# Expert feed-forward stages: the tile code rolled into hardware loops, rows staged by ScalarE, landings counted by SyncE, and the last stage's additions issued at other steps

## The chip, the cores and the metric

The kernel runs on one core of one Trainium2 chip. Its engines are TensorE (PE; PEld is its weight load), VectorE (DVE), ScalarE (ACT), GpSimd (POOL) and SyncE (SP), each with an instruction stream of its own; they meet through semaphores. The metric is device time in microseconds, lower is better; the median of three runs is what counts.

## The reference

A two-layer decoder on x of 64 x 64 tokens of 128 values (4096 tokens, so 32 token tiles of 128). Each layer is a sequence mixer, a cross attention and a mixture-of-experts feed-forward stage. Only the two feed-forward stages are touched:

```python
# layer 0: gate by sigmoid, two of eight experts, plus two shared experts
top_w = softmax(gathered);  h_r = gelu(x @ Wfc_r[e].T);  expert_out = h_r @ Wproj_r[e].T
return x + shared_out + routed_out
# layer 1, the last stage: gate by softmax, two of eight experts, with biases
for e in range(8):
    h = gelu(x @ W1[e] + b1[e]);  y = h @ W2[e] + b2[e]
    output = output + y * combine_w[..., e:e + 1]
```

## The kernel before

`ffn_phase` is built twice, as f0 (layer 0) and f1 (layer 1, the last stage). It sends every token row to its two experts by sorting:

- **Routing.** DVE works out for each token and choice the slot of its row. Slots are grouped in tiles of 128 rows, each tile owned by one expert (`owner[0, tile]`). Tokens are cut in two parts of 20 and 12 token tiles, which need 47 and 31 slot tiles: M = 78. `hot(q)` writes, for a group q of four token tiles, two one-hot arrays (`hot_tile`, times the token's number, and `hot_row`), and PE multiplies them (`collect(q)`) into the table `source` of rows by slot. Groups 0 to 4 belong to part 0. Groups 5 to 7 (part 1) are made at steps `HOT_LATER` of the tile loop.
- **Rows in.** POOL fetches 128 rows for each slot tile with an indirect DMA (`f_xn<-f_xn_rows,f_source`, L1616) into a ring of 32 tiles, in lots of 1, 1, 2 and then 4. A lot may start when the tile 32 places back has been read. Below, a *burst* is a run of such DMAs issued one behind the other.
- **Tile steps.** A Python loop over s = 0..79 writes out every step. PE transposes tile s (L1956), multiplies tile s-1 by the up weights (four matmuls, L1963) and tile s-2 by the down weights (four, L1975). DVE copies the transposed rows from PSUM (`xT`, L1797), adds the up bias in f1 (L1802), and writes y of tile s-2 (L1817; with its bias L1815 in f1). ACT does gelu (L1880) and copies the owner's up weights into a ring of three (`w_tile`, L1868). Each engine reads the tile's owner into a register with a TENSOR_LOAD (L1542) and addresses weights or biases by it.
- **Rows out.** SP stores y two tiles at a time. When part 0 is stored, POOL gathers the results back to token order, eight indirect DMAs for each group m (L1627, `f_hot_row<-f_slots_y,f_slots`), and DVE adds them with their weights (`add_rows`, L1560), in four quarters. Two buffers hold groups m and m+1, so the gather of group m+2 waits until group m is added. Groups 0 to 2 are added at steps `ADDED_AT` and the three after each, the others behind the loop. Group 5 is the first that needs part 1.

```python
        for s in range(M + 2):
            if s in lot_of: pe.wait_ge(landed[n], ...)   # PE itself waits for the lot's landing
            pe.transpose(bank_x[s % 2][:, 0:P], x_in[:, s % RING, :], g.ident[:])
HOT_LATER = (4, 10, 16)
ADDED_AT = (63, 69, 75)
```

Of the kernel before, what the change touches and what calls it, by code (L numbers as in the profile page):

```python
# [23 lines left out]
ALU = mybir.AluOpType  # L24
AXIS = mybir.AxisListType

P = 128
# [1305 lines left out]
W_RING = 3  # L1333
# [94 lines left out]
def ffn_phase(g, name, spec):  # L1428
# [14 lines left out]
    RING = TILES  # L1443
    lots = [(start[part] + begin, size) for part in range(parts)
            for begin, size in in_lots(counts[part], (1, 1, 2, 4) if part == 0 else (4,))]
    lot_of = {begin: n for n, (begin, _) in enumerate(lots)}
    stores = [(part, begin, size) for part in range(parts) for begin, size in in_lots(counts[part], (STORED,))]
    store_of = {start[part] + begin + t: n for n, (part, begin, size) in enumerate(stores) for t in range(size)}
    stores_of = [sum(1 for part, _, _ in stores if part < upto) for upto in range(parts + 1)]
    with ExitStack() as ctx:  # L1450
# [22 lines left out]
        def lent(n, shape, dt=F32):  # L1473

            if not following:
# [22 lines left out]
        xT = [sb(f"xT{k}", [D, P]) for k in range(2)]  # L1498
        w_tile = [sb(f"w_tile{k}", [D, FFN]) for k in range(W_RING)]
        hidden = [sb(f"hidden{k}", [P, FT, P]) for k in range(2)]  # L1500
        y_out = [sb(f"y_out{k}", [P, STORED, D]) for k in range(Y_RING)]
# [12 lines left out]
                 "owner_ready", "hot_ready", "hot_used", "source_ready", "xT_in_psum", "xT_ready",  # L1514
                 "w_ready", "up_done", "biased", "hidden_ready", "y_in_psum", "y_ready")
        S = {k: g.sem(f"{name}_{k}") for k in names}
        stored = [g.sem(f"{name}_y_stored{k}") for k in range(Y_RING)]
# [22 lines left out]
        def owner_of(kind, tile):  # L1540

            _, (value,) = nc.values_load_multi_w_load_instructions(  # L1542
                owner[0:1, tile:tile + 1], engines=(kind,), min_val=0, max_val=EXPERTS - 1,
                skip_runtime_bounds_check_because="a minimum with EXPERTS - 1 bounds them")
            return value
# [17 lines left out]
        def stores_done(eng, upto):  # L1563

            for k in range(Y_RING):
                need(eng, stored[k], 16 * len(range(k, upto, Y_RING)))

        statistics = RowStatistics(g, name, ctx)
        with nc.Block() as block:  # L1569

            @block.sync
            def _(sp):
# [6 lines left out]
                for n, (part, begin, size) in enumerate(stores):  # L1579
                    sp.wait_ge(S["y_ready"], start[part] + begin + size)  # L1580
                    sp.dma_start(slots_y[part].rearrange("(j p) d -> p j d", p=P)[:, begin:begin + size, :],
                                 y_out[n % Y_RING][:, 0:size, :]).then_inc(stored[n % Y_RING], 16)
# [10 lines left out]
                stores_done(sp, len(stores))  # L1593

            @block.gpsimd
            def _(pool):
# [5 lines left out]
                if spec["plus_xn"]:  # L1602
                    for q in range(GROUPS):
# [15 lines left out]
                for m in range(GROUPS):  # L1619
                    part = max(p for p in range(parts) if first_group[p] <= m)  # L1620
                    if m in first_group:
                        stores_done(pool, stores_of[part + 1])
# [10 lines left out]
            def _(dve):  # L1633
# [95 lines left out]
                def hot(q):  # L1729
# [7 lines left out]
                    seq(dve.tensor_tensor(out, tile_numbers[:, 0:N].unsqueeze(1).unsqueeze(1).to_broadcast(shape),  # L1737
                                          tile_of[:, :, at].unsqueeze(3).to_broadcast(shape), ALU.is_equal))
                    dve.tensor_tensor(out, out, token_rows[:, at].unsqueeze(1).unsqueeze(3).to_broadcast(shape),
                                      ALU.mult)  # L1740
# [51 lines left out]
                for s in range(M + 2):  # L1792
                    if biased and s < M:
                        held[s] = owner_of(mybir.EngineType.DVE, s)
                    if s < M:
                        dve.wait_ge(S["xT_in_psum"], s + 1)
                        dve.tensor_copy(xT[s % 2][:], bank_x[s % 2][:, 0:P]).then_inc(S["xT_ready"], 1)  # L1797
                    m = s - 1
                    if biased and 0 <= m < M:
                        dve.wait_ge(S["up_done"], m + 1)  # L1800
                        shape = [P, 1, FT, P]
                        dve.tensor_tensor(before_gelu[m % 2][:].unsqueeze(1),  # L1802
                                          bank_h[m % 2][:].rearrange("p (o j t) -> p o j t", o=1, t=P),
                                          b_up[:, bass.ds(held[m], 1), :].unsqueeze(3).to_broadcast(shape), ALU.add)\
                            .then_inc(S["biased"], 1)
                    m = s - 2
                    if 0 <= m < M:
                        dve.wait_ge(S["y_in_psum"], m + 1)
                        n = store_of[m]
                        at = m - start[stores[n][0]] - stores[n][1]  # L1810
                        if at == 0:
                            need(dve, stored[n % Y_RING], 16 * (n // Y_RING))
                        y, out = bank_y[m % 2][:, 0:D].unsqueeze(1), y_out[n % Y_RING][:, at:at + 1, :]
                        if biased:
                            ins = dve.tensor_tensor(out, y, b_down[:, bass.ds(held.pop(m), 1), :], ALU.add)  # L1815
# [3 lines left out]
                    if parts > 1 and s in HOT_LATER:  # L1819
                        hot(first_group[1] + HOT_LATER.index(s))  # L1820
                        if s == HOT_LATER[-1]:
                            sources(1)
                    if parts > 1:
                        for m, begin in enumerate(ADDED_AT):
# [258 lines left out]
```

## Time and profile before

| | us |
|---|---|
| median of 3 runs (1453.18 to 1457.63) | 1457.05 |
| the profiled execution, its own time | 1444.6 |
| its span, first instruction to last | 1442.8 |
| PE busy in it | 1175.6 (81%) |
| DVE busy | 829.6 (57%) |
| ACT busy | 649.3 (45%) |
| POOL busy | 600.1 (42%) |

The profiled execution is one run with the trace on; it lies 12.4 us under the median of the timed runs. Its span is what the rows below add up in. In these rows names are given without buffer numbers and without the digit of f0 and f1: f0's tile steps lie between 288 and about 515 us, f1's between 1139 and 1393 us.

### The profile page before, as it was taken

What the parts mean: (1) busy time and instruction counts of PE and PEld (TensorE: products, weight loads), DVE (VectorE), ACT (ScalarE), POOL (GpSimd) and SP (SyncE); (2) the same over time, 40 slices, a digit from 0 to 9 for tenths busy, and PEclk for the clock granted to TensorE, in tenths of its full rate; (3) what the DMA queues carried; (4) which work ended last, traced back from release to release, by engine and by line L of the source; (5) the groups of instructions that cost most, each with busy time, mean ns of one, the idle gap of its engine ahead of it and who ended that gap; (6) DMA issues with size and microseconds to landing.
All of it is one profiled execution on the core that took longest, in us unless ns stands there. A gap on an engine that the chain in (4) does not pass through costs nothing. (4 is left out here: it accounts for less than half of the span.)

```text
span 1442.8 us, 31655 instructions
## 1 busy us (share of the span) xinstructions
PE 1175.6 (81%) x11702; PEld 988.7 (69%) x11702; DVE 829.6 (57%) x1805; ACT 649.3 (45%) x1171; POOL 600.1 (42%) x622
## 2 busy tenths in 40 slices
PE   6979989919996889689999999968997718886840
PEld 4766666819996867468888888856767718885840
DVE  6859978403221324358888888847986615553541
ACT  5327754304453424155666656536772103452410
POOL 4742323264444235544343433333342463444255
PEclk9999998959997999899999999999997959997975
DMA  6002215012221121100000000001105011221122
GB/s 171 9 2 66 51 24 202 14 46 49 57 65 47 46 85 32 44 6 1 0 0 0 0 0 0 1 6 19 21 9 196 25 45 43 60 58 46 42 79 69
DMA packets 61906, 62.62 MB, mean 43 GB/s; under 512 B 12592, under 2 KB 50864, under 8 KB 61296
## 3 DMA queue, kind: packets, MB, share of 16 engines
q1 hardware_dynamic: 51824, 42.52, 9.9%
q0 software_dynamic: 9088, 18.63, 5.2%
q8 instruction: 61, 1.00, 0.3%
q14 instruction: 37, 0.30, 0.1%
q10 hardware_dynamic: 896, 0.17, 0.1%
HBM read 42.67 MB, written 16.52 MB: 41 GB/s over the span
## 5 line engine op out<-in xcount | busy, mean ns | idle before, releaser
L1963 PE MATMUL f_bank<-f_xT,f_w_tile 128*128 128x128 f32 x1248 | 184.5, 295 | 82.7 <-issue 48.1
L1963 PEld LDWEIGHTS f_bank<-f_xT,f_w_tile 128*128 128x128 f32 x1248 | 167.7, 208 | 88.9 <-issue 50.8
L1975 PE MATMUL f_bank<-f_w_down,f_hidden 128*128 x1248 | 179.2, 290 | 50.8 <-ACT f_hidden L1880 30.0
L1975 PEld LDWEIGHTS f_bank<-f_w_down,f_hidden 128*128 128x128 f32 x1248 | 162.6, 203 | 56.4 <-issue 56.2
L1616 POOL DMA_INDIRECT f_xn<-f_xn_rows,f_source x156 | 148.6, 952 | 47.4 <-issue 47.4
L1424 POOL TENSOR_TENSOR f_turn_cell<-ident 128x1 f32<-128x1 f32 x60 | 12.8, 213 | 319.5 <-issue 107.1
L1627 POOL DMA_INDIRECT f_hot_row<-f_slots_y,f_slots x128 | 122.6, 958 | 39.9 <-issue 39.9
L1050 POOL TENSOR_TENSOR ret_rstd<-ret_var,ret_minus_half 128x8 f32<-128x8 f32 x32 | 52.7, 1647 | 173.5 <-DVE ret_var L1089 173.5
L1880 ACT ACTIVATE f_hidden<-f_before_gelu 128x512 f32<-128x512 f32 x78 | 49.0, 629 | 162.0 <-DVE f_before_gelu L1802 146.4
L1880 ACT ACTIVATE f_hidden<-f_bank 128x512 f32<-128x512 f32 x78 | 46.5, 596 | 149.5 <-remote 83.9
L1868 ACT ACTIVATE f_w_tile<-f_w_up 128x512 f32 x156 | 96.2, 619 | 29.0 <-DVE f_owner L1768 28.2
L885 PEld LDWEIGHTS a_mixed_psum<-a_v_diag,a_probT 128*64 128x64 f32 x2048 | 65.8, 138 | 59.4 <-ACT a_probT L837 43.7
L1817 DVE COPY f_y_out<-f_bank 128x128 f32<-128x128 f32 x78 | 22.7, 291 | 138.9 <-PE f_bank L1975 100.0
L788 DVE TENSOR_REDUCE a_top<-a_scores 128x16 f32<-128x1024 f32 x64 | 78.4, 1224 | 37.5 <-PE a_scores L870 36.5
L747 POOL TENSOR_TENSOR X<-X,a_mixed 128x128 f32<-128x128 f32 x64 | 29.2, 456 | 160.6 <-DVE a_mixed L780 160.1
L837 ACT ACTIVATE a_probT<-a_probT_psum 128x1024 f32<-128x1024 f32 x64 | 65.5, 1024 | 57.6 <-PE a_probT_psum L896 57.6
L1053 POOL TENSOR_TENSOR ret_qk<-ret_qk,ret_turned 128x1024 f32<-128x1024 f32 x32 | 76.3, 2386 | 25.2 <-DVE ret_turned L1109 25.1
L1802 DVE TENSOR_TENSOR f_before_gelu<-f_bank,f_b_up 128x512 f32<-128x512 f32 x78 | 53.8, 689 | 52.0 <-PE f_bank L1963 28.9
L791 DVE TENSOR_TENSOR a_prob<-a_scores,a_top 128x1024 f32<-128x1024 f32 x64 | 78.4, 1224 | 2.2
L885 PE MATMUL a_mixed_psum<-a_v_diag,a_probT 128*64 128x18 f32 x2048 | 71.3, 212 | 7.9 <-ACT a_probT L837 5.9
L896 PE MATMUL a_probT_psum<-ident,a_prob 128*128 128x128 f32 x512 | 70.8, 282 | 5.9 <-ACT a_prob L811 5.9
L1258 PE MATMUL ret_ps<-ret_wo,ret_gated 128*128 128x128 f32 x512 | 67.1, 285 | 4.9 <-DVE ret_gated L1081 4.8
(283 smaller groups left out, 2827.8 us busy)
## 6 DMA issues: line engine op xcount, KB each, us to landing
f_slots_y<-f_y_out SPq DMA_DIRECT2D x76, 128.0 KB
a_v_rows<-in_ctx SPq DMA_DIRECT2D x16, 256.0 KB, 4.0
f_xn_rows<-f_xn SPq DMA_DIRECT2D x16, 256.0 KB
f_w_up<-in_f_up SPq DMA_DIRECT2D x1, 2560.0 KB, 10.1
f_w_down<-in_f_down SPq DMA_DIRECT2D x1, 2560.0 KB, 17.1
f_xn<-f_xn_rows,f_source POOLq DMA_INDIRECT x156
X<-in_x SPq DMA_DIRECT2D x4, 512.0 KB, 5.3
kv_ctxT<-in_ctxT SPq DMA_DIRECT2D x8, 256.0 KB, 5.7
```

The costliest lines, as they stand in the source:

```text
L788: dve.tensor_reduce(top[b][:], bank_s[b][:], AXIS.X, ALU.max).then_inc(S["top_ready"], 1)
L791: dve.tensor_tensor(prob[b][:], bank_s[b][:], top[b][:].unsqueeze(2).to_broadcast([P, HEADS, SEQ]), ALU.subtract)\
L885: last = pe.matmul(bank_o[64 * row:64 * row + 64, 18 * hp:18 * hp + 18], probT[b][:, hp, 64 * row:64 * row + 64], v_diag[octet][:, 2 * (tu ...
L896: last = pe.transpose(bank_t[:, hp, :], prob[b][:, 2 * hp:2 * hp + 2, :].rearrange("p h t -> p (h t)"), g.ident[:])
L1053: pool.tensor_tensor(qk[k % 2][:], qk[k % 2][:], turned[k % 2][:], ALU.add)\
L1258: last = pe.matmul(ps_vg[:, 0:D], gated[b][:, h, :], wo[:, h, :], start=(h == 0), stop=(h == H - 1))
L1616: pool.indirect_dma_start(out=x_in[:, s % RING, :], out_offset=None, in_=xn_rows[:, :], in_offset=bass.IndirectOffsetOnAxis(ap=source[:, s ...
L1627: pool.indirect_dma_start(out=rows[m % 2][:, t, n, :], out_offset=None, in_=slots_y[part][:, :], in_offset=bass.IndirectOffsetOnAxis(ap=sl ...
L1868: nc.scalar.activation(w_tile[s % W_RING][:].unsqueeze(1), w_up[:, bass.ds(expert + E0, 1), :], ACT.Copy)\
L1880: nc.scalar.activation(hidden[m % 2][:].rearrange("p j t -> p (j t)"), before_gelu[m % 2][:].rearrange("p j t -> p (j t)") if biased else ...
L1963: last = pe.matmul(bank_h[m % 2][:, j * P:(j + 1) * P], w_tile[m % W_RING][:, j * P:(j + 1) * P], xT[m % 2][:], start=True, stop=True)
L1975: last = pe.matmul(bank_y[m % 2][:, 0:D].unsqueeze(1), hidden[m % 2][:, j, :], w_down[:, bass.ds(expert + E0, 1), j, :], start=(j == 0), s ...
```

## The change

Both feed-forward stages write out only the first and last tile steps, and put those between them in loops on the engines: each engine's loop has a body of eight steps, and a loop counter in a register takes the place of the step number in waits and addresses. `DVE_LOOP` = (16, 56), `ACT_LOOP` = (8, 72), `PE_LOOP` = (16, 72) are the first step in the loop and the first behind it.

- In a loop the owners of eight tiles are read into eight registers by one TENSOR_LOAD (on PE and DVE one of four and one of eight for each pass; on ACT one of eight and one of one).
- A loop can't name a different landing semaphore at each step. SP now waits for each lot and adds its size to `rows_landed`; ACT waits on that, copies the rows of tile s+2 into a ring of four (`x_stage`), and PE transposes from there. POOL's ring waits on `x_staged` in place of the transpose.
- `w_tile` has two buffers, not three; ACT's order in a step is gelu, weights, rows (before: weights, gelu).
- y lies in one array of eight tiles; the pair that straddles the two parts is stored as two singles, the second behind the landing of the first.
- Groups 5 to 7 of `hot` at steps 4, 8, 12 (before 4, 10, 16), the second part's `source` at step 15.
- In f1 alone POOL makes the product of `hot_tile` for groups 0 to 4, and the additions of groups 0 to 3 stand at steps 58, 63, 68, 73 (before: groups 0 to 2 at 63, 69, 75). f0 keeps 63, 69, 75.

```diff
-W_RING = 3
+W_RING, X_RING = 2, 4
...
+        def over_tiles(eng, step, begin, end):
+            for s in range(begin):
+                step(s, s % BODY, s)
+            with eng.Fori(begin // BODY, end // BODY) as i:
+                for k in range(BODY):
+                    step(BODY * i + k, k, None, i)
+            for s in range(end, M + 2):
+                step(s, s % BODY, s)
...
+                for q in range(M // STORED):
+                    while ahead < len(lots) and lots[ahead][0] <= STORED * q + BODY:
+                        sp.wait_ge(landed[ahead], landed_base[ahead] + 16 * lots[ahead][1])
+                        sp.sem_inc(S["rows_landed"], lots[ahead][1])
+                        ahead += 1
...
+                for q in BY_POOL:
+                    pool.wait_ge(S["hot_tile_set"], q + 1)
+                    at, N = slice(GTILES * q, GTILES * (q + 1)), counts[0]
+                    shape, out = [P, TOP_K, GTILES, N], hot_tile[q % 2][:, :, :, 0:N]
+                    pool.tensor_tensor(out, out, token_rows[:, at].unsqueeze(1).unsqueeze(3).to_broadcast(shape),
+                                       ALU.mult).then_inc(S["hot_tile_ready"], 1)
-                    waits = [(S["source_ready"], part_of[begin] + 1), (S["xT_in_psum"], begin + size - RING)]
+                    waits = [(S["source_ready"], part_of[begin] + 1), (S["x_staged"], begin + size - RING)]
...
+                            act.wait_ge(S["rows_landed"], s + t + 1)
+                            need(act, S["xT_in_psum"], s + t - X_RING + 1)
+                            nc.scalar.activation(x_stage[(k + t) % X_RING][:].unsqueeze(1), x_in[:, bass.ds(slot, 1), :],
+                                                 ACT.Copy).then_inc(S["x_staged"], 1)
...
-                            pe.wait_ge(landed[n], landed_base[n] + 16 * lots[n][1])
-                        pe.transpose(bank_x[s % 2][:, 0:P], x_in[:, s % RING, :], g.ident[:])\
+                        pe.wait_ge(S["x_staged"], s + 1)
+                        pe.transpose(bank_x[k % 2][:, 0:P], x_stage[k % X_RING][:], g.ident[:])\
...
-HOT_LATER = (4, 10, 16)
-ADDED_AT = (63, 69, 75)
+HOT_LATER, SOURCES_AT = (4, 8, 12), 15
+DVE_LOOP, ACT_LOOP, PE_LOOP = (16, 56), (8, 72), (16, 72)
```

How the change moves instructions is seen at three places. The first is ACT in f0, in mid-stage; before, a step is weights (L1868), gelu (L1880) and one owner read:

```order
L1868 ACTIVATE f0_w_tile2<-f0_w_up 128x512
L1880 ACTIVATE f0_hidden0<-f0_bank0 128x512 [waits f0_y_in_psum,f0_up_done]
L1542 TENSOR_LOAD f0_owner
L1868 ISA [waits f0_up_done]
L1868 ACTIVATE f0_w_tile0<-f0_w_up 128x512
L1880 ACTIVATE f0_hidden1<-f0_bank1 128x512 [waits f0_y_in_psum,f0_up_done]
```

The same place after the change, at the head of ACT's loop body (L1931 is gelu, L1922 the weights, L1951 the staged rows, and the TENSOR_LOAD reads eight owners):

```order
L1553 ISA
L39 REGISTER_ALU [waits f0_up_done]
L1931 ACTIVATE f0_hidden1<-f0_bank1 128x512 [waits f0_y_in_psum]
L1541 ISA
L1541 TENSOR_LOAD f0_owner
L1922 ISA [waits f0_up_done]
L1922 ACTIVATE f0_w_tile1<-f0_w_up 128x512
L1949 REGISTER_ALU
L39 REGISTER_ALU [waits f0_rows_landed]
L1951 ISA [waits f0_xT_in_psum]
L1951 ACTIVATE f0_x_stage2<-f0_xn 128x128
```

The read of eight stands behind the gelu and ahead of the weights and the rows that PE needs next. The second place is DVE in f1, after the change, the first two steps of its loop body (L1850 is the copy of the transposed rows, L1855 the up bias, L1867 y); before, each step had one read of one owner ahead of its L1797:

```order
L1553 ISA
L1541 TENSOR_LOAD f1_owner
L1849 REGISTER_ALU
L1850 COPY f1_xT0<-f1_bank2 128x128
L1855 ISA
L1855 TENSOR_TENSOR f1_before_gelu1<-f1_bank1,f1_b_up 128x512
...
L1867 TENSOR_TENSOR f1_y_out<-f1_bank4,f1_b_down 128x128
L1541 ISA
L1541 TENSOR_LOAD f1_owner
L1849 REGISTER_ALU
L1850 COPY f1_xT1<-f1_bank3 128x128
```

The first read is of four owners and the second of eight; both stand ahead of the copy of the transposed rows and of the bias. The third place is POOL in f1 after the change, between the constants and the first fetch of rows:

```order
L1631 MEMSET f1_per_tile 128x320
L1642 TENSOR_TENSOR f1_hot_tile0<-f1_hot_tile0,f1_token_rows 128x376
L1642 TENSOR_TENSOR f1_hot_tile1<-f1_hot_tile1,f1_token_rows 128x376
L1642 TENSOR_TENSOR f1_hot_tile0<-f1_hot_tile0,f1_token_rows 128x376
L1642 TENSOR_TENSOR f1_hot_tile1<-f1_hot_tile1,f1_token_rows 128x376
L1642 TENSOR_TENSOR f1_hot_tile0<-f1_hot_tile0,f1_token_rows 128x376
L1425 TENSOR_TENSOR f1_turn_cell<-ident 128x1
```

The five products are new here; before, DVE made them (L1739), and POOL went from its constants to the first fetch.

## Rows read from the trace of the kernel before

**Rows 1.** The page: span, and in section 5 one GpSimd product.

```profile
span 1442.8 us, 31655 instructions
...
L1053 POOL TENSOR_TENSOR ret_qk<-ret_qk,ret_turned 128x1024 f32<-128x1024 f32 x32 | 76.3, 2386 | 25.2 <-DVE ret_turned L1109 25.1
```

**Rows 2.** Stretches (from:to, length, busy us and instructions, PEclk, DMA share, GB/s).

```profile
core 0: us, PE busy (x) PEld busy (x) DVE busy (x) ACT busy (x) POOL busy (x), PEclk, DMA share, GB/s
278.00:324.00 46.00, 14.89 (x91) 12.29 (x89) 5.33 (x16) 4.14 (x8) 32.87 (x42) 0.68 0.17 46
...
700.00:900.00 200.00, 199.94 (x2397) 167.71 (x2396) 167.72 (x296) 121.22 (x216) 80.73 (x40) 1.00 0.00 0
```

**Rows 3.** Timeline of f1 in steady work (start us, us, engine, line, operation).

```profile
1263.87 0.27 PE L1956 MATMUL f_bank<-ident,f_xn 128*128 128x128 f32 x1
...
1264.18 0.29 DVE L1815 TENSOR_TENSOR f_y_out<-f_bank,f_b_down 128x128 f32<-128x128 f32 x1 [0.66 <-PE f_bank L1975]
...
1265.18 0.69 DVE L1802 TENSOR_TENSOR f_before_gelu<-f_bank,f_b_up 128x512 f32<-128x512 f32 x1 [0.34 <-PE f_bank L1963]
...
1265.87 1.06 PE L1963 MATMUL f_bank<-f_xT,f_w_tile 128*128 128x128 f32 x8
1265.90 0.63 ACT L1880 ACTIVATE f_hidden<-f_before_gelu 128x512 f32<-128x512 f32 x1 [1.20 <-DVE f_before_gelu L1802]
...
1266.44 0.61 ACT L1868 ACTIVATE f_w_tile<-f_w_up 128x512 f32 x1
...
1266.77 1.06 PE L1975 MATMUL f_bank<-f_w_down,f_hidden 128*128 x8
...
1267.66 0.27 PE L1956 MATMUL f_bank<-ident,f_xn 128*128 128x128 f32 x1
```

**Rows 4.** Timeline of f0: the same parts of a step.

```profile
464.75 0.60 ACT L1880 ACTIVATE f_hidden<-f_bank 128x512 f32<-128x512 f32 x1 [0.78 <-PE f_bank L1963]
...
467.34 0.27 PE L1956 MATMUL f_bank<-ident,f_xn 128*128 128x128 f32 x1
```

**Rows 5.** Line L1542, owner reads: duration ns min/median/max.

```profile
L1542 ACTq TENSOR_LOAD <-f_owner x156: 271/278/503, 281.3 to 1379.5; - x156
L1542 DVEq TENSOR_LOAD <-f_owner x78: 298/303/552, 1142.7 to 1384.8; - x78
```

**Rows 6.** Timeline at the front of f0 and at one later round of gathers.

```profile
307.17 0.69 DVE L1407 TENSOR_TENSOR X<-f_bank,X 128x512 f32<-128x512 f32 x1 [24.79 <-remote]
...
318.38 0.94 POOL L1616 DMA_INDIRECT f_xn<-f_xn_rows,f_source  x1 [0.30 <-issue]
...
323.91 0.60 ACT L1880 ACTIVATE f_hidden<-f_bank 128x512 f32<-128x512 f32 x1 [40.31 <-remote]
...
398.40 0.60 ACT L1880 ACTIVATE f_hidden<-f_bank 128x512 f32<-128x512 f32 x1 [2.61 <-remote]
```

**Rows 7.** Timeline of f1: group 2's burst, and the transposes around it.

```profile
1352.55 0.27 PE L1956 MATMUL f_bank<-ident,f_xn 128*128 128x128 f32 x1
...
1352.55 0.96 POOL L1627 DMA_INDIRECT f_hot_row<-f_slots_y,f_slots  x1 [0.45 <-issue]
...
1368.68 0.42 PE L1956 MATMUL f_bank<-ident,f_xn 128*128 128x128 f32 x1
```

**Rows 8.** Timelines: part 0's last y and the turn behind it; f1's tail.

```profile
431.72 0.29 DVE L1817 COPY f_y_out<-f_bank 128x128 f32<-128x128 f32 x1 [1.41 <-PE f_bank L1975]
...
434.50 0.19 POOL L1424 TENSOR_TENSOR f_turn_cell<-ident 128x1 f32<-128x1 f32 x1 [6.05 <-DMA f_slots_y<-f_y_out]
...
1392.16 0.19 POOL L1424 TENSOR_TENSOR f_turn_cell<-ident 128x1 f32<-128x1 f32 x1 [9.54 <-issue]
...
1393.10 0.29 DVE L1815 TENSOR_TENSOR f_y_out<-f_bank,f_b_down 128x128 f32<-128x128 f32 x1 [1.07 <-PE f_bank L1975]
...
1432.16 0.95 POOL L1627 DMA_INDIRECT f_hot_row<-f_slots_y,f_slots  x1 [0.30 <-issue]
```

**Rows 9.** Timeline of f1's first `hot`: the product that moves to POOL.

```profile
1121.89 0.55 DVE L1739 TENSOR_TENSOR f_hot_tile<-f_hot_tile,f_token_rows 128x376 f32<-128x376 f32 x1
```

More of the change, by code:

```diff
@@ L1443, in ffn_phase @@
     RING = TILES
+    BY_POOL, ADDED_AT = range(first_group[1]) if spec["last"] else (), spec["added_at"]
     lots = [(start[part] + begin, size) for part in range(parts)
             for begin, size in in_lots(counts[part], (1, 1, 2, 4) if part == 0 else (4,))]
[L1446 to L1449, printed above, removed]
+    seams = [q for q in range(M // STORED) if any(STORED * q < at < STORED * (q + 1) for at in start)]
     with ExitStack() as ctx:
@@ L1791, in _, with step, owned @@
                 held = {}
[L1792 to L1795, printed above, removed]
+                def step(s, k, tile, i=None):
+                    if biased and tile is None:
+                        if k == 0:
+                            held.update(zip(range(-4, 0), owners(mybir.EngineType.DVE, s - 4, 4)))
+                        if k == 1:
+                            held.update(zip(range(BODY), owners(mybir.EngineType.DVE, s - 1, BODY)))
+                    elif biased:
+                        for t in (tile - 2, tile - 1, tile):
+                            if 0 <= t < M and (t, "tail" if tile >= DVE_LOOP[1] else "head") not in held:
+                                held[t, "tail" if tile >= DVE_LOOP[1] else "head"], = owners(mybir.EngineType.DVE, t)
+                    def owned(back):
+                        return held[k - back] if tile is None else held[tile - back, "tail" if tile >= DVE_LOOP[1] else "head"]
+                    if live(s, M):
@@ L1814, in _ @@
                         if biased:
-                            ins = dve.tensor_tensor(out, y, b_down[:, bass.ds(held.pop(m), 1), :], ALU.add)
+                            ins = dve.tensor_tensor(out, y, b_down[:, bass.ds(owned(2), 1), :], ALU.add)
                         else:
@@ L1818, in _ @@
                         ins.then_inc(S["y_ready"], 1)
[L1819 to L1824, printed above, removed]
-                            if s in range(begin, begin + 4):
-                                add_rows(dve, m, s - begin)
+                    if tile in HOT_LATER:
+                        hot(first_group[1] + HOT_LATER.index(tile))
+                    if tile == SOURCES_AT:
+                        sources(1)
+                    for m, begin in enumerate(ADDED_AT):
+                        if tile is not None and tile in range(begin, begin + 4):
+                            add_rows(dve, m, tile - begin)
+                over_tiles(dve, step, *DVE_LOOP)
                 for m in range(GROUPS):
@@ L1883, in _ @@
+                over_tiles(act, step, *ACT_LOOP)
                 if shared:
```

165 lines of the change are left out of this document (100 added, 65 removed).

## The prediction

> **What bounds the kernel now.** I read the page first for the span, 1442.8 us [rows 1], then the timelines of f0 and f1, since only these two stages change. In steady work PE sets the pace. In f1 one transpose is recorded at 1263.87 and the next but one at 1267.66 [rows 3]: 3.79 us for two steps, 1.90 us each, in which PE has no gap. DVE and ACT stand waiting in brackets ([... <-PE], [... <-DVE]), so what they do in a step is hidden as long as it ends before PE wants it. At 1.90 us, 78 tiles would take 148 us in each stage.
>
> They take much longer, and the second view says why. At the front of f0, DVE waits 24.79 us and ACT 40.31 us for something "remote", until 307.17 and 323.91; POOL issues its indirect fetches one behind the other until 318.38 [rows 6]. In 278 to 324 PE is busy for 14.89 of 46 us at a clock of 0.68, while POOL is busy for 32.87 [rows 2]. What the engines wait for is work that PE has recorded as done: PE's completions reach them late while POOL issues a long burst, and come through some us behind it. A round of four fetches does it on a small scale (ACT waits 2.61 us until 398.40 [rows 6]). Group 2's gather in f1 shows the price of a burst of eight: POOL starts it at 1352.55, and PE goes from the transpose at 1352.55 to the fourth one behind it at 1368.68, 16.1 us where four steps take 7.6 [rows 7]. So a burst of eight inside the tile loop costs **8.5 us**. Behind the loop PE has nothing to do and POOL alone is the path: from its turn at 1392.16 to its last gather's end at 1433.1 lie four groups, 10.2 us each [rows 8].
>
> **The bursts.** The change issues as many indirect DMAs as before, in the same lots. The ring's condition moves from the transpose to the staged copy, which comes a step earlier, but POOL still runs 32 fetches at each stage's front without waiting. I leave those waits as they are: 0 us. Were they halved, 78 tiles of f0 alone would gain some 15 us, which is a rival below.
>
> **Owner reads in the loops.** Today each step reads one owner, 0.278 us on ACT and 0.303 on DVE [rows 5]. In the loops one instruction reads eight. Its time isn't in this trace. From below it is that of a single read, 0.3 us; from above eight of them, 2.3. I take 1.8, nearer the upper end, since eight words of memory are fetched and only a fixed part can be shared. What lies behind it:
>
> - ACT in f1. Gelu starts at 1265.90 and the weights' copy at 1266.44 today [rows 3]. With 1.8 for the read and 0.1 for the address the copy starts at 1267.8, and the staged rows, issued 0.54 behind it and taking about 0.3, are ready at 1268.65. PE wants them for the transpose at 1267.66: 1.0 us late.
> - DVE in f1. The read of eight can start when y is dispatched, 1264.18 [rows 3]. Then the copy of the transposed rows ends at 1266.4 (PE wants it for the matmuls at 1265.87), the bias at 1267.1 and gelu at 1267.7, and PE wants gelu's result for the down matmuls at 1266.77: 0.9 late. This is the step behind ACT's, and both delays fall on the same transpose, so the larger counts, not their sum.
> - ACT in f0, where no bias stands between: gelu at 464.75, rows at 467.45, transpose at 467.34 [rows 4]: 0.1 late.
> - PE's own read of eight is in the middle of an up product; its sequencer runs about a us ahead, and I add nothing.
>
> ACT's loop has eight passes. In f1 two of them lie where PE waits for bursts anyway, so 6 x 1.0 = **6 us**; in f0 8 x 0.1 = **1 us**. With 2.3 us for the read the two are 9 and 5; with 0.3 they are 0. The Trainium skill (Runtime: NRT & Kernel Launch, section Instruction fetch mechanics) gives about 200 ns a register for such a load, "even for bulk"; by that the read of eight would be an estimated 1.6 us and these two terms together about 5 us. This trace shows single reads alone.
>
> **Additions in f1.** Groups 0 to 2 are added at 58, 63 and 68 in place of 63, 69 and 75, and group 3 at 73. So the gathers of groups 2 and 3 start some steps earlier, and group 4's, which today starts at 1392.16 as the third addition ends [rows 8], moves into the loop. The loop then holds a third burst of eight at 8.5, where today group 3's, at the loop's end, costs much the same. PE's last product, and with it the last y (1393.10 [rows 8]), comes 8.9 us later (8.5, and 0.4 for a full price of group 3's). The tail shrinks from four groups to three, minus 10.2. But today the tail's first gather starts 0.9 us ahead of the last y; now it is group 5's, which needs all of part 1 stored. In f0 the last y of part 0 starts at 431.72 and POOL's turn behind its store comes at 434.50: 2.8 us [rows 8]. So 0.9 + 2.8 = 3.7 are added. Sum: 8.9 + 3.7 - 10.2 = **+2.4 us**. If the fourth burst costs PE nothing this is -6.5; if the additions, three steps apart in the shadow of the bursts, cost 3 us more, +5.
>
> **POOL's product.** DVE's 0.55 us in `hot_tile` [rows 9] goes; POOL, at 2.39 us for 1024 elements in a row [rows 1], takes about 0.9 for 376, beside DVE's comparison of rows. It shortens the first group; behind it PE's collecting sets the pace. **-0.5 us**, between -0.6 and +0.5.
>
> **At nothing.** ACT's third copy: gelu and weights are issued 0.54 apart [rows 3], so a step takes 0.54 + 0.54 + about 0.3 = 1.4 of 1.90; if PE's step were below 1.4 it would bound. SP's count of landings: lots are fetched up to 32 tiles ahead. SP's wait at the seam: its store queue has a ring of eight tiles behind it. Branches: in 700 to 900, inside a loop of another stage, PE is busy for 199.94 of 200 us [rows 2]. Earlier `hot` steps: three of the same size as before, 0 +- 1.
>
> **Sum.** 6 + 1 + 2.4 - 0.5 = 8.9 us. The profiled execution would go from 1444.6 to 1453.5. It lies 12.4 under the median of the runs shown, and I carry the same difference to the median: 1457.05 + 8.9 = **1466 us**.
>
> **Rivals.**
>
> - *Faster, by the additions.* The place is group 4's gather, now inside f1's loop. PE's late completions are counted by time, not by burst; with three bursts close together the third may hide in waits that PE has anyway. It decides once that burst costs PE less than 6 us while the owner reads cost under 1: -6.5 - 0.5 = -7, 1450 us. For it: ACT and DVE wait on PE alone. Against: the price of 8.5 is for one burst out of two that PE met separately. Chance 0.17.
> - *Faster, by the waits moved out of PE.* Today PE itself waits for landings (its transposes at the front of each stage), and its completions may be held up behind that wait and not by POOL; SP's count would free them, f0's front of 46 us and f1's alike. Half of each would be some 20 + 20 us: 1417. Against: the wait until 398.40 [rows 6] is in mid-lot, where PE waits for no landing. Chance 0.08.
> - *No change.* A read of eight costs little more than one: 2.4 - 0.5 = +2, 1459 us. For it: it is one instruction. Chance 0.32.
> - *Code is fetched again at each loop's end.* 1490 us or so, if each of 7 passes of PE and 8 of ACT in two stages cost 1 to 2 us. The loop of another stage shows none: 700 to 900 has a DMA share of 0.00 and PE at 199.94 [rows 2]. Chance 0.03. The Trainium skill (Runtime, Instruction fetch mechanics) says that a taken branch whose target isn't in the two blocks held "forces a DMA fetch"; by that rule a body of eight steps, if over two blocks long, would pay at each pass. The trace of that other loop doesn't show it.
> - *My forecast*, slower by 5 us or more through reads and bursts: chance 0.37. The rest, 0.03, is faster by something that I don't see.
>
> **How the numbers follow.** About 0.3% (4.4 us) is what a measurement of this kernel tells from no change. Faster: 0.17 + 0.08 + 0.03 = 0.28. Within: 0.32. Slower: 0.37 + 0.03 = 0.40. Low end: the reads at 0 and the fourth burst hidden, -7, and 2 us of spread in the runs: 1448. High end: reads at 14, additions at +5, spread 4: 1480. Outside lie the case of the moved waits, the fetched code and some of the forecast's own tail.
>
> **What would show it.** Owner reads (TENSOR_LOAD at L1541) in the loops of 1.6 us or more, against singles of 0.3, and behind them, every eighth tile, a transpose spacing of 2.9 in f1 and 2.0 in f0; if the reads take 0.3, that term fell. DVE's and ACT's remote waits at the stages' fronts as long as before, 25 and 40 us; if they are gone, the second rival holds. In f1 three bursts of eight between the 16 and the loop's end, each with some 8 us of late transposes, and three groups, not four, behind the last y. A spacing of 1.9 through the fourth burst would show the first rival. What would make it wrong beyond these: a different length of the waits behind bursts, since they total far more than anything that I add.

## The result, and the profile after

| | us |
|---|---|
| median of 4 runs (1465.41 to 1472.42) | 1469.04 |
| the kernel before, beside it | 1455.74 |
| ratio, 95% interval | 1.0092 (1.0057 to 1.0127) |
| the profiled execution, its own time / its span | 1466.5 / 1464.7 |

The kernel became 13.3 us slower (13.4 by the ratio, 8 to 18 by its interval). The forecast was 1466, slower by 8.9.

One warning first. The kernel before takes 1442.5, 1443.8 or 1456.5 us, according to the job it runs in (they ran on different chips). The trace behind [rows 1 to 9] is of an execution of 1444.6, the changed kernel's of 1466.5. The 21.9 us between their spans is therefore the change and the chip together. Ratios are used only within a job, and stages are compared only between traces of jobs in which the kernel before takes the same time.

The page of the changed kernel:

```profile
span 1464.7 us, 32478 instructions
PE 1181.9 (81%) x11702; PEld 989.6 (68%) x11703; DVE 824.2 (56%) x1801; ACT 680.2 (46%) x1328; POOL 610.5 (42%) x627
```

ACT is busy 31 us longer (156 staged copies) and POOL 10 us, 8.6 of it the five products; PE has 6 us more and DVE 5 less.

The owner reads of the changed kernel in the middle of f1, by line (duration ns min/median/max). Here each eight steps have one read of one and one of eight on ACT, one of four and one of eight on PE and DVE:

```profile
L1541 ACTq TENSOR_LOAD <-f_owner x8: 282/416/555, 1232.9 to 1297.5; - x8
L1541 PEldq TENSOR_LOAD <-f_owner x8: 330/472/728, 1233.6 to 1297.6; - x8
L1541 DVEq TENSOR_LOAD <-f_owner x8: 344/485/615, 1234.2 to 1298.3; - x8
```

Of these the longest are the reads of eight: here about 0.55 us on ACT and 0.6 on DVE, against 0.28 and 0.30 for a single one [rows 5]. In f0's loop ACT's take longer, up to 0.79. I had taken 1.8. The Trainium skill (Runtime: NRT & Kernel Launch, section Instruction fetch mechanics) gives about 200 ns a register "even for bulk", on a page that describes such a load as one of registers from HBM; these owners lie in SBUF. Here seven more registers cost 0.3 us, some 40 ns each, and in f0's loop up to 0.5 us; the rows decide.

The forecast named a second sign, a spacing of 2.9 us between transposes at every eighth tile of f1. It is not there. Outside the rounds of fetches and the bursts, f1's spacings in this trace are 1.90 except at nine places, mostly just behind the heads of the loops, that are 0.1 to 0.5 us longer, 2.0 us in all; the same kernel without loops (e3) has 0.3 us of this kind.

The front of f0 in the changed kernel, from ACT's and DVE's timelines:

```profile
317.24 0.69 DVE L1408 TENSOR_TENSOR X<-f_bank,X 128x512 f32<-128x512 f32 x1 [36.94 <-remote]
...
322.17 0.60 ACT L1931 ACTIVATE f_hidden<-f_bank 128x512 f32<-128x512 f32 x1 [38.51 <-PE f_bank L2037]
```

The long waits of [rows 6] are still there. A landing counted by SP, and a PE that no longer waits for it, did not free PE's completions. The rival of the moved waits falls.

The first of f1's three bursts of eight (group 2's gather), from the timeline, around the transposes of tiles 65 and 66:

```profile
1368.26 0.27 PE L2030 MATMUL f_bank<-ident,f_x_stage 128*128 128x128 f32 x1
...
1369.05 1.44 PE L2037 MATMUL f_bank<-f_xT,f_w_tile 128*128 128x128 f32 x8 [0.52 <-DVE f_xT L1850]
...
1373.18 0.95 POOL L1663 DMA_INDIRECT f_hot_row<-f_slots_y,f_slots  x1 [0.31 <-issue]
1375.30 0.69 DVE L1855 TENSOR_TENSOR f_before_gelu<-f_bank,f_b_up 128x512 f32<-128x512 f32 x1 [6.30 <-remote]
...
1378.74 0.42 PE L2030 MATMUL f_bank<-ident,f_x_stage 128*128 128x128 f32 x1
```

PE's up product (L2037) is recorded as ended at 1370.5; DVE, which waits for it, goes on at 1375.30, 1.2 us behind the end of POOL's last fetch. From one transpose to the next are 10.48 us in place of 1.90. The three bursts of eight (groups 2, 3 and 4) lose 9.5, 8.1 and 7.3 us of PE's time (transpose spacings above 1.90, summed over five, five and two tiles), as the forecast had it (8.5). Behind the loop:

```profile
1421.82 0.29 DVE L1867 TENSOR_TENSOR f_y_out<-f_bank,f_b_down 128x128 f32<-128x128 f32 x1 [1.50 <-PE f_bank L2057]
...
1424.22 0.20 POOL L1425 TENSOR_TENSOR f_turn_cell<-ident 128x1 f32<-128x1 f32 x1 [13.87 <-DVE X L1572]
...
1454.08 0.95 POOL L1663 DMA_INDIRECT f_hot_row<-f_slots_y,f_slots  x1 [0.30 <-issue]
```

POOL's turn comes 2.4 us behind the last y, and three groups take 30.8 us, where four stood before [rows 8]. This part of the forecast can be read off as it was written. It does not say where 13 us come from, since the reads cost next to nothing.

### The profile page after: what moved, and what is told of

Read it like the earlier page. It is cut to its first block and busy times, and to the rows that moved or that the text cites. A ratio compares the mean times of both kernels' runs of the same rounds, so it can differ in the third digit from the quotient of the medians.

```text
span 1464.7 us, 32478 instructions
## 1 busy us (share of the span) xinstructions
PE 1181.9 (81%) x11702; PEld 989.6 (68%) x11703; DVE 824.2 (56%) x1801; ACT 680.2 (46%) x1328; POOL 610.5 (42%) x627
## 5 line engine op out<-in xcount | busy, mean ns | idle before, releaser
L2037 PE MATMUL f_bank<-f_xT,f_w_tile 128*128 128x128 f32 x1248 | 183.6, 294 | 85.7 <-issue 46.5
L2037 PEld LDWEIGHTS f_bank<-f_xT,f_w_tile 128*128 128x128 f32 x1248 | 166.6, 207 | 93.0 <-issue 49.3
L1931 ACT ACTIVATE f_hidden<-f_before_gelu 128x512 f32<-128x512 f32 x78 | 49.1, 629 | 159.5 <-DVE f_before_gelu L1855 143.7
L1931 ACT ACTIVATE f_hidden<-f_bank 128x512 f32<-128x512 f32 x78 | 46.4, 595 | 143.0 <-PE f_bank L2037 111.9
L1922 ACT ACTIVATE f_w_tile<-f_w_up 128x512 f32 x156 | 96.5, 620 | 31.6 <-DVE f_owner L1807 28.3
L1855 DVE TENSOR_TENSOR f_before_gelu<-f_bank,f_b_up 128x512 f32<-128x512 f32 x78 | 53.7, 688 | 76.9 <-remote 43.1
## 6 DMA issues: line engine op xcount, KB each, us to landing
f_xn_rows<-f_xn SPq DMA_DIRECT2D x16, 256.0 KB, 13.3
```

Source lines behind the costliest of these rows:

```text
L1922: nc.scalar.activation(w_tile[b][:].unsqueeze(1), w_up[:, bass.ds(expert + E0, 1), :], ACT.Copy)\
L1931: nc.scalar.activation(hidden[b][:].rearrange("p j t -> p (j t)"), before_gelu[b][:].rearrange("p j t -> p (j t)") if biased else bank_h[b ...
L2037: last = pe.matmul(bank_h[b][:, j * P:(j + 1) * P], w_tile[(k - 1) % W_RING][:, j * P:(j + 1) * P], xT[b][:], start=True, stop=True)
```

## The experiments

The kernels of a job share its runs of the kernel before. A difference in us behind a ratio is the ratio's, times the kernel before of its job; the medians' own difference can lie 1 to 3 us beside it. The diffs show the changed part of a line. "Lost" is, in f0 or f1, the time from the first transpose of its 78 tiles to the last, less 77 times 1.896 us, the spacing in steady work. Most of it is waiting; some 6 us of f1's are PE's own products for groups 5 to 7, about 2 us each.

**e1, additions alone.** The kernel before, f1's additions where the change puts them:

```diff
-ADDED_AT = (63, 69, 75)
+ADDED_ALL = {False: (63, 69, 75), True: (58, 63, 68, 73)}
```

> The kernel before with only f1's additions at 58, 63, 68, 73. Theory A (the additions' new third burst costs PE about what the tail saves): between -1 and +4 us against the kernel before; three groups behind the last y in place of four, last y some 9 to 14 us later. Theory B (additions are the loss of the whole change): +8 to +13 us. Theory C (additions gain, the rolled code loses all): -4 us or less.

Measured: 1444.18 against 1442.5, ratio 1.0015 (0.9999 to 1.0030), +2.2 us. In f1 the transposes lose 108.6 us in place of 96.4, and behind the last transpose 49.8 us remain in place of 61.6. Theory A; the new burst costs about what the tail gives back.

**e2, additions taken back** in the changed kernel.

```diff
-added_at=(58, 63, 68, 73)
+added_at=(63, 69, 75)
```

> The changed kernel with f1's additions back at 63, 69, 75. Theory A: within 3 us of the changed kernel, so some 11 to 13 us above the kernel before. Theory B: the time of the kernel before, +0 to +3 us. Theory C: slower than the changed kernel, +16 us or more above the kernel before.

Measured: 1454.43, ratio 1.0087 (1.0058 to 1.0116): 12.5 us above the kernel before, so the loss is not the additions'. f1 loses 103.4 us, 7.0 more than before with the same additions.

**e3, no loops.** The changed kernel, each step written out with one owner read.

```diff
-DVE_LOOP, ACT_LOOP, PE_LOOP = (16, 56), (8, 72), (16, 72)
+DVE_LOOP = ACT_LOOP = PE_LOOP = (80, 80)
```

> The changed kernel with no loops: every step written out, with one owner read per step; staged rows, two weight buffers, SP's count and the additions stay. Theory L (the loops themselves cost, by reads of eight at 0.6 us and branches): 5 us or more faster than the changed kernel. Theory R (the loss sits in the shorter rings and ACT's third copy, which leave less work ahead of PE when a completion comes late): within 3 us of the changed kernel, and each round of four gathers in f0 still costs some 1.8 us where it cost 1.0 before.

Measured: 1457.31, ratio 1.0092 (1.0063 to 1.0122), the changed kernel's own. The loops, their reads and branches cost nothing that these times can tell. The two ratios come from different jobs and each has an interval of 0.3%, so the times alone would leave room for some 6 us; the spacings behind the loop heads, 2.0 us in f1 with loops and 0.3 without, narrow that. Each round of four fetches in f0 costs 1.4 to 1.5 us here, less than the 1.8 expected and more than the 1.0 of before. The loss stays in what the change did besides.

**e4, 12 tiles ahead.** The kernel before; the ring keeps its 32 tiles, but a lot is fetched only when the tile 12 back is transposed.

```diff
-(S["xT_in_psum"], begin + size - RING)
+(S["xT_in_psum"], begin + size - AHEAD)     # AHEAD = 12
```

> The kernel before, with POOL's fetches of rows held to 12 tiles ahead of the transposes in place of 32; the ring of 32 stays. Theory P (PE's completions reach the other engines late while POOL issues a burst, about 1.25 us for each fetch of it): the stall at each stage's front shrinks from 32 fetches to 12, so 20 to 25 us less in each stage, and some five rounds more at 1.0 us in f0 and 1.9 in f1: 25 to 40 us faster than before. Theory W (what holds PE up at the fronts is its own wait for landings or the start of the stage): no gain, -2 to +5 us.

Measured: 1416.07, ratio 0.9813 (0.9785 to 0.9840), 27 us faster. The fronts of f0 and f1, in windows of e4 (columns as in [rows 2]):

```profile
278.00:324.00 46.00, 35.57 (x281) 34.66 (x280) 11.26 (x34) 14.81 (x27) 21.71 (x28) 0.89 0.16 45
1128.00:1182.00 54.00, 42.22 (x315) 40.54 (x314) 28.10 (x68) 21.49 (x36) 26.62 (x34) 0.87 0.18 51
```

and the same in e9, the kernel before again:

```profile
278.00:324.00 46.00, 14.20 (x95) 13.27 (x94) 3.04 (x9) 4.39 (x8) 30.11 (x39) 0.62 0.17 45
1137.00:1191.00 54.00, 16.90 (x86) 15.41 (x87) 11.52 (x29) 8.69 (x14) 34.29 (x44) 0.59 0.18 45
```

PE, which waits at the front for the same landings in both, is busy for 35.6 in place of 14.2 us of 46 once POOL's burst is 12 fetches and not 32. That it waits there itself isn't what holds it up; how many fetches POOL issues in a row is. Part of the gain was given back: POOL's last lots and part 0's 16 gathers now follow each other at tiles 65 to 70, which lose 27.9 us in f0 and 27.5 in f1 (before: the gathers at 53 to 60, 16.9 and 18.6).

**e5, the changed kernel again**, with e6 to e8.

> The changed kernel once more, on the chip of the next three, as their measure. Some 12 to 14 us above the kernel before.

Measured: 1469.99 against 1456.49, 13.5 us above; ratio 1.0103 (1.0071 to 1.0135), 15.0 us.

**e6, ACT's work ahead in f1.** Four weight buffers, and weights and rows copied ahead of gelu (between the two calls stand the owner, the weights of s+1 and the rows of s+2).

```diff
+        W_RING = 4 if spec["last"] else 2
...
+                    if not biased:
+                        gelu_step()
...
+                    if biased:
+                        gelu_step()
```

> The changed kernel with f1's weight ring of four in place of two, and in f1 ACT copies weights and rows ahead of gelu (f0 as it is). Theory R (the loss is that ACT has less work done ahead when a completion of PE comes late): f1's tiles 24 to 48 lose some 4 us again, as before the change, in place of 7 to 8 a half, and the whole is 5 to 8 us faster than the changed kernel. Theory S (the loss is the staged copy itself, a chain of one more engine between the landing and PE): within 2 us of it.

Measured: 1467.17, ratio 1.0066 (1.0047 to 1.0084), 5.4 us better than e5 by the ratios and 2.8 by the medians, but the intervals meet. Tiles 24 to 48 of f1 lose 15.4 us in place of 17.8, while all of f1 loses 121.2 in place of 119.4 in the two profiled executions. Unclear.

**e7, hot_tile's product on DVE again.**

```diff
-    BY_POOL, ADDED_AT = range(first_group[1]) if spec["last"] else (), spec["added_at"]
+    BY_POOL, ADDED_AT = (), spec["added_at"]
```

> The changed kernel with the product of hot_tile on DVE for all groups, as before the change. Theory F (POOL's five products stand ahead of its first fetch, and make f1's front 1.5 us longer): 1 to 2 us faster, and from the last attention to f1's first transpose 52.0 us in place of 53.5. My prediction's term: 0.5 us slower.

Measured: 1468.33, ratio 1.0082 (1.0069 to 1.0095), 3 us better than e5, again within its interval. From the last attention's end to POOL's first fetch it is 49.2 us here. Over all traces it is 49.2 to 49.7 in the seven where DVE makes the product and 49.4 to 49.8 in the seven where POOL does, 0.1 us apart on average. So moving the product neither cost nor gained anything that can be told, although one takes POOL 1.73 us (L1642 of the changed kernel) and not the 0.9 of the forecast. And the front did not come down to 52.0, it stayed at 53.5. Its excess has another cause (e10).

**e8, two weight buffers** in the kernel before.

```diff
-W_RING = 3
+W_RING = 2
```

> The kernel before with two weight buffers in place of three, nothing else. Theory R: slower than before by 4 to 9 us, in the rounds of four gathers of both stages. Theory S: within 2 us of the kernel before.

Measured: 1464.45, ratio 1.0049 (1.0035 to 1.0064), +7 us (5 to 9), as theory R had it. One round of it in f1:

```profile
1291.26 0.63 ACT L1868 ACTIVATE f_w_tile<-f_w_up 128x512 f32 x1 [0.97 <-PE f_bank L1963]
...
1297.03 0.63 ACT L1868 ACTIVATE f_w_tile<-f_w_up 128x512 f32 x1 [2.43 <-remote]
...
1298.22 0.63 ACT L1880 ACTIVATE f_hidden<-f_before_gelu 128x512 f32<-128x512 f32 x1 [0.56 <-DVE f_before_gelu L1802]
```

With two buffers the weights wait for a completion of PE at each step, and gelu stands behind them. The buffer matters in this order of ACT's; whether it does in the changed kernel's, which has gelu first, e10 shows.

**e9, the kernel before again**, on the chip of e10 to e12.

> The kernel before, unchanged, for a profile on the chip of the next three. If the earlier difference of 14 us between chips lies in f0's and f1's late completions, f0's 78 tiles lose some 76 us on a chip where the kernel takes 1442 and some 86 where it takes 1456.

Measured: 1443.03, ratio 1.0005. f0 loses 77.5 us, f1 96.7, as in the trace of before. The 86 for a chip where it takes 1456 was not measured: there only kernels with changed stages were profiled (f0 lost 87.2 us in e8, whose buffers account for an unknown part of that).

**e10, no staged rows.** e3, with PE transposing from the landed rows and waiting for the lots itself; SP doesn't count, ACT doesn't copy, and POOL's ring waits on the transpose again.

```diff
...
-                    waits = [(S["source_ready"], part_of[begin] + 1), (S["x_staged"], begin + size - RING)]
+                    waits = [(S["source_ready"], part_of[begin] + 1), (S["xT_in_psum"], begin + size - RING)]
...
-                        pe.wait_ge(S["x_staged"], s + 1)
-                        pe.transpose(bank_x[k % 2][:, 0:P], x_stage[k % X_RING][:], g.ident[:])
+                        if n is not None:
+                            pe.wait_ge(landed[n], landed_base[n] + 16 * lots[n][1])
+                        pe.transpose(bank_x[k % 2][:, 0:P], x_in[:, s % RING, :], g.ident[:])
```

> The changed kernel unrolled, and PE transposing straight from the landed rows and waiting for their landing itself, as before the change: no staged copy, no count by SP. Two weight buffers, gelu ahead of weights, hot at 4, 8, 12 and the additions stay. Theory S (the staged copy is the loss): 4 to 8 us faster than the changed kernel, first fetch to first transpose in f1 2.7 us in place of 4.3. Theory R (weight buffers and ACT's order): 2 us of that only, and the rounds of four in f1 still cost over 2.5 us each.

Measured: 1446.76 against 1443.8, ratio 1.0027 (1.0013 to 1.0041). e3 had 1.0092 (1.0063 to 1.0122), in a job in which the kernel before takes 1442.5. The two intervals don't meet. The staging is worth 0.65%, **9.4 us** (5 to 14 by the two intervals, more than theory S named), by far the largest part of the loss. "Staging" is three things here, which no run parts: the count by SP, the copy by ACT, and the ring's wait on the copy. POOL's turns in the middle of f1 show the cost of a round (start, and in brackets how long POOL had waited for the ring). In e9, the kernel before:

```profile
1262.53 0.19 POOL L1424 TENSOR_TENSOR f_turn_cell<-ident 128x1 f32<-128x1 f32 x1 [4.12 <-PE f_bank L1956]
1271.95 0.19 POOL L1424 TENSOR_TENSOR f_turn_cell<-ident 128x1 f32<-128x1 f32 x1 [4.08 <-PE f_bank L1956]
1281.41 0.19 POOL L1424 TENSOR_TENSOR f_turn_cell<-ident 128x1 f32<-128x1 f32 x1 [4.11 <-PE f_bank L1956]
```

In e10, without staging:

```profile
1263.27 0.19 POOL L1425 TENSOR_TENSOR f_turn_cell<-ident 128x1 f32<-128x1 f32 x1 [4.06 <-PE f_bank L2021]
1272.67 0.19 POOL L1425 TENSOR_TENSOR f_turn_cell<-ident 128x1 f32<-128x1 f32 x1 [4.05 <-PE f_bank L2021]
1282.09 0.19 POOL L1425 TENSOR_TENSOR f_turn_cell<-ident 128x1 f32<-128x1 f32 x1 [4.07 <-PE f_bank L2021]
```

In e3, with staging and otherwise the same:

```profile
1261.38 0.19 POOL L1425 TENSOR_TENSOR f_turn_cell<-ident 128x1 f32<-128x1 f32 x1 [5.47 <-ACT f_x_stage L1952]
1271.32 0.19 POOL L1425 TENSOR_TENSOR f_turn_cell<-ident 128x1 f32<-128x1 f32 x1 [4.59 <-ACT f_x_stage L1952]
1282.08 0.19 POOL L1425 TENSOR_TENSOR f_turn_cell<-ident 128x1 f32<-128x1 f32 x1 [5.41 <-ACT f_x_stage L1952]
```

Four tiles take 9.4 us in the first two and 9.9 to 10.8 in the third; without late completions they would take 7.6. At the front of f1, first fetch and first transpose in e10:

```profile
1135.54 1.06 POOL L1649 DMA_INDIRECT f_xn<-f_xn_rows,f_source  x1 [0.16 <-issue]
...
1138.23 0.30 PE L2021 MATMUL f_bank<-ident,f_xn 128*128 128x128 f32 x1 [0.31 <-DMA f_xn<-f_xn_rows,f_source]
```

and in e3:

```profile
1142.15 1.06 POOL L1653 DMA_INDIRECT f_xn<-f_xn_rows,f_source  x1 [0.16 <-issue]
...
1146.03 0.60 ACT L1952 ACTIVATE f_x_stage<-f_xn 128x128 f32<-128x128 f32 x2
...
1146.47 0.65 PE L2031 MATMUL f_bank<-ident,f_x_stage 128*128 128x128 f32 x2 [1.93 <-issue]
```

2.7 us and 4.3: the way over SP and ACT is 1.6 us longer, and nothing hides it there. All seven traces with staging have 4.3, all seven without it 2.7 to 2.8.

The rest lies in the rounds of four fetches. Tiles 24 to 48, which hold six of them, lose 18.6 us in e3's f1 against 11.7 in e10's, and 9.3 against 5.7 in f0; the front's burst and the bursts of gathers, where most of the waiting is, cost the same with and without staging to within 1.5 us each. What a round does can be seen in f0. In e10 the last transpose ahead of it and its first fetch:

```profile
387.22 0.27 PE L2021 MATMUL f_bank<-ident,f_xn 128*128 128x128 f32 x1
...
388.31 0.96 POOL L1649 DMA_INDIRECT f_xn<-f_xn_rows,f_source  x1 [0.45 <-issue]
```

and in e3, with the round's end:

```profile
389.47 0.27 PE L2031 MATMUL f_bank<-ident,f_x_stage 128*128 128x128 f32 x1
...
391.06 0.96 POOL L1653 DMA_INDIRECT f_xn<-f_xn_rows,f_source  x1 [0.45 <-issue]
...
397.52 1.15 PE L2058 MATMUL f_bank<-f_w_down,f_hidden 128*128 x8 [0.72 <-ACT f_hidden L1932]
...
397.79 0.30 ACT L1952 ACTIVATE f_x_stage<-f_xn 128x128 f32<-128x128 f32 x1
...
398.51 0.27 PE L2031 MATMUL f_bank<-ident,f_x_stage 128*128 128x128 f32 x1
```

The late transpose at 398.51 doesn't wait for its copy, which is done at 398.09; it stands behind the down product, which waits for gelu. In e3's f0 no transpose starts less than 0.4 us behind the end of its copy. At the front of f1, where PE does wait for the copy, it is 0.05 to 0.14. What differs is where in PE's step the round starts. With the ring on the transpose, the first fetch of each full round in these tiles comes 1.09 us behind a transpose, in e9 and e10, f0 and f1. With the ring on the copy it comes elsewhere, in the changed kernel at two points in turn:

| first fetch behind a transpose | a round of four costs |
|---|---|
| f0, 1.09 us (e9, e10) | 1.0 us |
| f0, 1.59 (e3, and the changed kernel in turn) | 1.4 to 1.6 |
| f0, 2.05 (the changed kernel in turn) | 1.9 to 2.0 |
| f1, 1.09 (e9, e10) | 1.8 to 1.9, one 2.4 |
| f1, 1.64 (the changed kernel in turn) | 2.5 |
| f1, 2.1 to 2.2 (the changed kernel in turn) | 2.9 to 3.1 |

The later in the step, the dearer the round, about us for us. This speaks for the ring's wait, and not for the time of the copy. It is no proof: in e2's f0 two rounds that start at 2.04 cost 0.4 only, and e3's f1 lies above this line. A kernel with staged rows and the ring on the transpose would tell; none was run.

**e11, paced fetches** in the kernel before: a short front, then a lot of five each four tiles, then the gathers in halves of four, one each four tiles. The front was meant to be 12 rows; by the edit it is 17, since the lot that begins at tile 12 waits for 4 * (12 - 12) // 5 = 0 tiles.

```diff
-(1, 1, 2, 4) if part == 0 else (4,)
+(1, 1, 2, 4, 4, 5) if part == 0 else (5,)
-(S["xT_in_psum"], begin + size - RING)
+(S["xT_in_psum"], max(begin + size - RING, 4 * (begin - 12) // 5))
-                    turn(pool, (added[1], GTILES * (m - 1)), (S["hot_used"], GROUPS))
                     for t in range(GTILES):
+                        if t % 2 == 0:
+                            at = GATHERS_AT[m][t // 2] if m < len(GATHERS_AT) else M
+                            turn(pool, (added[1], GTILES * (m - 1)), (S["hot_used"], GROUPS), (S["xT_in_psum"], at))
-ADDED_AT = (63, 69, 75)
+ADDED_AT, GATHERS_AT = (59, 67, 75), ((51, 55), (59, 63), (67, 71), (75, 78))
```

> The kernel before with all of POOL's fetches in both stages spread over the tile steps: 12 rows at the front, then lots of five, one each four tiles, then part 0's gathers in halves of four, one each four tiles, additions at 59, 67, 75. Theory P (the loss comes from long bursts, and a round with a gap behind it costs 1 to 3 us): 40 to 65 us lost in each stage in place of 76 and 96, so 1385 to 1410 on a chip where the kernel before takes 1442. Theory W' (each fetch costs PE the same wherever it stands): no better than the run with 12 ahead, 0.981 of before.

Measured: 1400.46, ratio 0.9717 (0.9687 to 0.9747), **41 us faster than the kernel before**, the best of all. f0 loses 54.6 us in place of 77.5. f1 loses 82.0 in place of 96.7, more than expected: its rounds of five cost 3.7 us each on average over tiles 24 to 48, and f0's 2.3. One of them, POOL's turn and fifth fetch, from POOL's timeline:

```profile
1199.41 0.19 POOL L1424 TENSOR_TENSOR f_turn_cell<-ident 128x1 f32<-128x1 f32 x1 [4.23 <-PE f_bank L1958]
...
1205.06 0.94 POOL L1616 DMA_INDIRECT f_xn<-f_xn_rows,f_source  x1 [0.30 <-issue]
```

PE's timeline there, the last transpose under the burst and the next one:

```profile
1204.66 0.27 PE L1958 MATMUL f_bank<-ident,f_xn 128*128 128x128 f32 x1
...
1209.81 0.27 PE L1958 MATMUL f_bank<-ident,f_xn 128*128 128x128 f32 x1
```

From one transpose to the next are 5.15 us. The gathers and the front pay, by 31 us each over both stages, and the rounds of five take 18 back. Tiles 48 to 77, under bursts of 16 and 8 gathers, lose 27.0 us in e9's f0 and 30.8 in its f1; under halves of four they lose 9.9 and 17.2. Tiles 0 to 16 lose 40.6 and 48.8 in e9, 26.1 and 32.1 here, and 16.0 and 18.1 in e4, whose front is 12 fetches. e4's front with these gathers was not run.

**e12, the same pacing in the changed kernel**, with the lots, halves and additions of e11.

```diff
-(S["x_staged"], begin + size - RING)
+(S["x_staged"], max(begin + size - RING, 4 * (begin - 12) // 5))
...
```

> The same pacing in the changed kernel, both stages. Theory R (less work ahead at every round): the change's loss grows with the number of rounds, so 12 to 20 us slower than the paced kernel before. If the staging helped at the front: within 5 us of it.

Measured: 1420.25, ratio 0.9846 (0.9818 to 0.9874). The change costs 1.3%, 19 us (13 to 25), in the paced kernel. That is more than the 13 to 15 it costs unpaced, but within its interval, so that it grows with the number of rounds isn't shown. Theory R's size; its cause is not the buffers if what e10 shows of the unpaced kernel holds here, which no run tests.

## Why the prediction was right, and where it was not

The time was met (1469 against 1466, 13.3 against 8.9 slower), but by luck: of the 8.9, 7 stood on a cost that measured 1 to 2, and a cost of 9.4 that the sum held at nothing took its place. Term by term:

- **Owner reads, +7 (6 + 1): wrong.** The step that failed is "I take 1.8, nearer the upper end, since eight words of memory are fetched and only a fixed part can be shared". The rows say 0.54 to 0.79, and e3, which has no read of eight and no loop, takes as long as the changed kernel (1.0092 both). With 0.3 to 0.6 for the read the forecast's own sum gives 0 for the term; the spacings behind the loop heads of f1 put 1 to 2 us in its place.
- **Staging at nothing: wrong, and the main cause.** Two steps failed. One is "SP's count of landings: lots are fetched up to 32 tiles ahead": at a stage's first tiles nothing is fetched ahead, and the way over SP and ACT is 1.6 us longer there. The other is of the ring's condition, which "moves from the transpose to the staged copy, which comes a step earlier, but POOL still runs 32 fetches at each stage's front without waiting. I leave those waits as they are: 0 us". That looks at the front alone. In the rounds of four behind it POOL's first fetch now comes at another point of PE's step, and the rounds cost 6.9 us more in f1 and 3.6 in f0 (e3 against e10, tiles 24 to 48). What was said of ACT's third copy, "0.54 + 0.54 + about 0.3 = 1.4 of 1.90", holds for steady work, in which the changed kernel runs at 1.90, and in e3's rounds in f0 PE doesn't wait for the copy either. That staging as a whole costs 9.4 us is shown by e3 and e10. (Their two profiled executions lie 14.1 apart: 6.5 in f1's tiles, 3.6 in f0's, 1.6 at f1's front, the rest elsewhere.) That in the rounds it does so through the ring's wait is argued from the traces, not shown.
- **Additions, +2.4: right.** e1 gives +2.2 (-0.1 to +4.3). Each piece was there as well: three bursts of eight at 7.3 to 9.5, 2.4 us to the turn, three groups in the tail.
- **POOL's product, -0.5: not there.** POOL takes 1.73 us for one, not 0.9; its first fetch comes within 0.1 us of where it came before, on average over the traces; and e7's 3 us lie inside e5's interval.
- **The long bursts themselves, 0: right.** The long waits stand as before. For the rounds of four the 0 was wrong, as said.
- **Two weight buffers, at nothing: right for this order only.** e10 has them and its ratio of 1.0027 is 0.12% from e1's, the kernel before with the same additions, and the intervals of the two meet; with weights ahead of gelu (e8) they cost 7.

Sum as measured: staging 9.4, additions 2.2, and 1.7 between e1 and e10 (buffers, ACT's order, `hot` steps and the product together, within noise), 13.3; reads and loops, at 0 by the times and 1 to 2 by f1's spacings, lie inside the intervals.

The first rival (the third burst of eight, group 4's, hides) fell with its 7.3 us, where it needed less than 6; the moved waits fell with the front; "no change" was right in its reason, the cheap read, and wrong in its time, since it too held staging at nothing; the fetched code fell with e3.

Left open: what in the chip holds PE's completions back while POOL issues indirect DMAs. e4 and e11 show that it does so with the length of the run of fetches, not why. The amount of data moved doesn't tell the two fronts apart, 45 GB/s in e4's f0 and in e9's. Open is also which of staging's three parts costs the rounds. That rounds alternate (in e3's f1 between 9.9 and 10.8 us, in the changed kernel's between 10.0 and 10.6) goes with the point of the step at which the first fetch comes, which alternates too. e3's f1 also runs at a clock of 0.92 in 1248 to 1290, where e10 has 1.00.

## What to carry to other kernels

When a wait moves to another semaphore, ask what it releases and at which point of the step, and not only whether the new link fits into the slack: the staged copy fitted, and the path that it came with still cost 9.4 us. Price a new link at a stage's start by itself, where nothing is fetched ahead. If completions come late while GpSimd issues indirect DMAs in a row, shorten the runs before tuning anything else; a ring of 32 tiles filled at once cost more than it hid, 12 ahead gave 1.9%, and 17 at the front with gaps behind it and halved gathers 2.8%. When a forecast meets the time, test its terms one by one all the same.

## What the runs showed of the hardware

- A load of eight registers from SBUF takes 0.54 to 0.79 us on ACT, 0.58 to 0.78 on PE and 0.60 to 0.62 on DVE, against about 0.3 for one.
- PE's completions against the length of a run of fetches: rounds of four cost 1.0 us in f0 and 1.9 in f1, of five 2.3 in f0 and 3.7 in f1 on average (e11), runs of eight 7.3 to 9.5, the 32 of a front 41 in f0 and 49 in f1 (tiles 0 to 16 of e9, with some 4 us of PE's products for groups 5 and 6 in each). In f1, from four to eight, the cost grows faster than the length.
- A round of four costs more the later in PE's step it starts: in f0 1.0 us at 1.09 us behind a transpose, 1.4 to 1.6 at 1.59 and 1.9 to 2.0 at 2.05 (with two rounds of e2 as exceptions), in f1 1.8 to 1.9 at 1.09 and 2.5 to 3.1 at 1.64 to 2.2.
- The granted clock follows: 0.59 to 0.62 in e9's fronts, where PE is busy a third of the time, 0.87 to 0.89 in e4's.
- The same kernel took 1442.5, 1443.8 and 1456.5 us in three jobs; the one percent between them is as large as the effect studied.
